# A graph layer in five stages: one block with a wait per engine in place of a barrier per stage, and one product placed ahead of a turn

## The reference, cut to what matters

```python
xn = _layernorm(x, axis=-1)
x = x + _L0_gnn_ref(xn, edge_index, ...) + _L0_mix_ref(xn[None], ...)[0]
x = x + _L0_ffn_ref(_layernorm(x, axis=-1)[None], ...)[0]
```

```python
phi_q = jnp.exp(jnp.einsum('bhnd,md->bhnm', q, rf) - q_norm)
phi_k = jnp.exp(jnp.einsum('bhnd,md->bhnm', k, rf) - k_norm)
kv = jnp.einsum('bhnm,bhnd->bhmd', phi_k, v)
numerator = jnp.einsum('bhnm,bhmd->bhnd', phi_q, kv)
attn = numerator / jnp.maximum(denominator, 1e-06)
return out @ proj_w.T + proj_b
```

```python
h = (x @ W).reshape(N, H, C)
e = jax.nn.leaky_relu(al_s[src] + al_d[dst], NEG_SLOPE)
alpha = ex / (denom[dst] + 1e-16)
out = jax.ops.segment_sum(h[src] * alpha[:, :, None], dst, num_segments=N)
h = jax.nn.elu(_gat_layer(x, src, dst, W1, ..., concat=True))
out = _gat_layer(h, src, dst, W2, ..., concat=False)
```

## Time and profile before

| | us |
|---|---|
| median of three runs | 2076.1 |
| lowest, highest | 2069.36, 2077.42 |
| the profiled execution | 2073.2 |
| its span | 2071.3 |

### The profile page before, as it was taken

One profiled execution on the slowest core, in us unless ns is written; L12 is line 12 of the kernel. 1 busy time (PEld: TensorE's weight loads), 2 busy tenths in 40 slices (PEclk: granted clock), 3 DMA queues, 4 the chain that ended last, 5 costly groups with the idle time before them and its releaser, 6 DMA issues. The chain is left out here.

```text
span 2071.3 us, 32352 instructions
## 1 busy us (share of the span) xinstructions
PE 1986.8 (96%) x9933; PEld 1467.1 (71%) x9934; DVE 1167.3 (56%) x2548; ACT 447.5 (22%) x822; POOL 185.0 (9%) x181
## 2 busy tenths in 40 slices
PE   5999899998999999999999999999989999999998
PEld 3666666666648887888888755556646777777876
DVE  6666436662566654888888642266863334343343
ACT  3222221222002321222222200013321222122222
POOL 0000000000000000000000000010002323233232
PEclk9999999999999999999999999999987999999999
DMA  8000220002644442732424234544126888899654
GB/s 262 18 17 20 93 108 17 17 19 75 219 144 149 151 128 73 221 124 86 139 91 137 68 146 155 182 125 157 49 75 227 247 270 258 228 286 281 177 137 84
DMA packets 81191, 282.78 MB, mean 137 GB/s; under 512 B 11689, under 2 KB 32225, under 8 KB 71490
## 3 DMA queue, kind: packets, MB, share of 16 engines
q1 hardware_dynamic: 59138, 211.02, 30.5%
q0 software_dynamic: 14848, 56.18, 11.3%
q10 hardware_dynamic: 7104, 14.26, 2.0%
HBM read 217.43 MB, written 63.99 MB: 136 GB/s over the span
## 5 line engine op out<-in xcount | busy, mean ns | idle before, releaser
L1402 PE MATMUL gat_Z<-h_head,first_rest 125*125 125x256 f32 (+1 forms) x1600 | 354.4, 380 | 3.9 <-DVEq L1302 3.9
L1402 PEld LDWEIGHTS gat_Z<-h_head,first_rest 125*125 125x125 f32 x1600 | 297.1, 188 | 49.7 <-issue 4.2
L777 PE MATMUL mix_G<-mix_w,xnT 128*125 128x384 f32 x720 | 246.3, 493 | 3.3 <-PEq L387 2.0
L777 PEld LDWEIGHTS mix_G<-mix_w,xnT 128*125 128x125 f32 x720 | 134.2, 191 | 89.4 <-issue 8.1
L2423 DVE TENSOR_SCALAR ex_idS<-ex_ids 128x1 int32 x52 | 8.0, 153 | 211.4 <-DMA out_rows<-ex_y,ex_idS 211.4
L2510 PE MATMUL ex_PH<-ex_xT,w_and_experts 128*128 128x128 f32 x936 | 113.4, 281 | 1.8 <-issue 0.9
L2510 PE MATMUL ex_PH<-ex_xT,ex_w 128*128 128x128 f32 x936 | 110.9, 277 | 0.5 <-issue 0.2
L2510 PEld LDWEIGHTS ex_PH<-ex_xT,w_and_experts 128*128 128x128 f32 x936 | 108.8, 195 | 2.8 <-issue 2.8
L2520 PE MATMUL ex_PY<-w_and_experts,ex_hT 128*128 128x384 f32 x312 | 107.5, 494 | 0.7 <-ACT ex_hT L2457 0.5
L2520 PE MATMUL ex_PY<-ex_w,ex_hT 128*128 128x384 f32 x312 | 107.3, 494 | 0.8 <-ACT ex_hT L2457 0.6
L2510 PEld LDWEIGHTS ex_PH<-ex_xT,ex_w 128*128 128x128 f32 x936 | 106.5, 192 | 0.7 <-issue 0.7
(11 more groups left out here) (400 smaller groups left out, 3096.2 us busy)
## 6 DMA issues: line engine op xcount, KB each, us to landing
w_and_experts<-in_L_ffn_W SPq DMA_DIRECT2D x32, 1152.0 KB, 8.9
ex_w<-in_L_ffn_W SPq DMA_DIRECT2D x32, 1152.0 KB, 8.5
first_wide<-c_dram SPq DMA_DIRECT2D x40, 546.9 KB
h1T_dram<-gat_oT ACTq DMA_DIRECT2D x40, 250.0 KB, 2.0
mix_w<-in_L_mix_qkv_w SPq DMA_DIRECT2D x6, 1152.0 KB, 12.8
ct_dram<-mix_count_out SPq DMA_DIRECT2D x40, 157.0 KB, 2.1
mix_w_slice<-in_L_gnn_W SPq DMA_DIRECT2D x6, 1024.0 KB, 12.3
proj_w2s<-in_L_gnn_W SPq DMA_DIRECT2D x4, 1536.0 KB, 9.2
```

The source lines that it names most:

```text
L777: last = pe.matmul(G[c][:], xnT[:, k, t * P:(t + 1) * P], w[:, k, c, :], start=(k == 0), stop=(k == KD - 1))
L1402: last = pe.matmul(Z[b][j][:], wt[b][:, s, :], h[hd][0:P, s, j * HC:(j + 1) * HC + j], start=(s == 0), stop=(s == NT - 1))
```

## The change

The stages from the first mixing half to the second projection stand in one block. The barriers and the empty block between them are gone; where one engine needs another's work, a wait on a semaphore stands on that engine. Eight PSUM banks (`bank[j]`) are named once, and each stage uses views of them. Both mixing halves and their numerators become one function. The norm, routing and expert stages keep their own blocks.

Other edits come with it:

- SP starts the second half's weights as soon as the first half's q, k and v are out of PSUM, part by part, and the projection's weights likewise behind the second half; it starts the second half's W1 slices when the first half's numerators are made;
- `phiq` lies over the W1 slices;
- PE's wait for `kv` stands behind the features of the queries, ahead of `R`;
- in the projection, a turn of a tile in the first half of the nodes waits for all numerators but the last; only the second tile's product waits for the last one;
- DVE makes the next stage's weights of tile 0 right after the second tile sum of the last pair in the first layer, and leaves the slopes of tile 1 to the next stage; the bias row is waited for at the first normalisation, no longer ahead of the first scores;
- semaphores are given back by POOL in `gat1_phase` and at the start of `gat2_route_phase`;
- a class `SecondStart` holds what the second projection needs first. DVE makes `T1`, `S` and one difference before it normalises the last tile (`first_sums`), and PE makes the second projection's first product ahead of the aggregation's last turn (`first_product`). `T1` lies in space of `h` there, and ACT copies it to where it is needed later.

```diff
-def numerator(nc, cx, tag, half, rfT, qT, kv, attn, load_next):
...
-        block = st.enter_context(nc.Block(no_gpsimd_drain=True))
...
+    @block.sync
+    def _(sp):
...
+        for half in range(2):
+            if half:
+                sp.wait_ge(num, 4 + SUMS)
+            for k in range(KH):
+                row = (half * KH + k) * 128
+                sp.dma_start(ws[k], gnn_w1[row:row + 128, :]).then_inc(slice_loaded[k], 16)
...
+            for c, (done, evac) in enumerate(((q_done, q_evac), (k_done, k_evac), (v_done, v_evac))):
+                sp.wait_ge(done, NT * (half + 1))
+                sp.wait_ge(evac, NT * (half + 1))
+                if half == 0:
+                    load_second(sp, c)
+            if half == 1:
+                load_proj(sp)
...
+        def numerators(half):
+            pe.wait_ge(s_evac, PER * NT * (half + 1))
+            with pe.Fori(0, HH // 2) as i:
+                for b in range(2):
+                    for j in range(6):
+                        m, c = j // CH, j % CH
+                        pe.wait_ge(q_exped, i * 12 + (FEATS * half + 6 * b + j + 1))
+                        pe.matmul(F[j][:, 0:CHW[c]], rfT[:, m * 128:(m + 1) * 128],
...
+                pe.wait_ge(kv_copied, 2 * (half + 1))
+                for b in range(2):
+                    pe.wait_ge(q_exped, i * 12 + (FEATS * half + 6 * b + 12))
...
 def proj_phase
...
         def _(sp):
+            sp.wait_ge(num, 4 + SUMS)
...
             def turn(t):
                 b = t % 2
+                pe.wait_ge(num_used, 2 + SUMS - (1 if t < NT // 2 else 0))
...
+                    elif t == 1:
+                        pe.wait_ge(num_used, 2 + SUMS)
...
 def first_layer_phase
...
+            sp.wait_ge(wa2_step, 2 * KF)
             load_w(0)
...
+            pool.wait_ge(projected, 2 * NT)
+            pool.wait_ge(summed, 2 * NT)
             pool.memset(large[:], BIG).then_inc(consts, 1)
...
                 tile_of(n, c22, p5_done, 1, 1, Y5)
                 if n == PAIRS - 1:
-                    slopes()
+                    weights(0)
...
-                if n == PAIRS - 1:
-                    weights(0)
...
+            pe.wait_ge(summed, 2 * NT)
             first(0)
...
 def gat1_phase
...
         def _(sp):
+            sp.wait_ge(p3_done, PAIRS)
             sp.dma_start(brow[:], b1.partition_broadcast(128)).then_inc(b_loaded, 16)
...
+            pool.wait_ge(p3_done, PAIRS)
+            cx.release(done_with)
...
-            dve.sem_inc(mn_ready, 2)
+            step(dve.scalar_tensor_tensor(u, u, SLOPE, u, ALU.mult, ALU.max))
             dve.tensor_tensor(e[1], u, rows[0][0:P, 1:2, P:2 * P].to_broadcast([P, NT, P]), ALU.subtract
                               ).then_inc(e_ready, 1)
-            dve.wait_ge(b_loaded, 16)
...
+                    if last and t == NT - 1:
+                        second.first_sums(dve)
                     normalise(hd, t)
...
+            pe.wait_ge(m_copied, 3)
+            pe.wait_ge(x_kept, 3 * PAIRS)
+            pe.wait_ge(ones_set, H1)
             aggregate(0, 0)
...
                     elif not last:
                         aggregate(hd + 1, 0)
+                    else:
+                        second.first_product(pe)
                     turn(hd, t)
...
 def gat2_project_phase
...
+            sp.wait_ge(turned1, H1 * NT + 2)
+            sp.wait_ge(t_evac1, H1 * NT + 2)
             load_pair(1)
...
+            dve.wait_ge(t1_kept, 1)
             dve.tensor_tensor(T4, B(1, 0), T2, ALU.subtract).then_inc(t_ready, 1)
...
+            act.wait_ge(t_ready, 1)
+            act.wait_ge(done, H1 * NT + 2)
+            act.activation(T1[:], second_start.T1, ACT.Copy).then_inc(t1_kept, 1)
...
+            pe.wait_ge(turned1, H1 * NT + 2)
             for n in range(HT):
-                first(n)
+                if n >= 1:
+                    first(n)
                 second(n)
...
+class SecondStart:
...
+    def first_sums(self, dve):
+        dve.wait_ge(self.ext_ready, 2)
+        dve.wait_ge(self.w_loaded, 128)
+        dve.tensor_tensor(self.T1, self.B(0, 1), self.B(0, 0), ALU.subtract).then_inc(self.t_ready, 1)
+        dve.wait_ge(self.first_loaded, 32)
+        dve.tensor_tensor(self.S, self.A(1, 0), self.A(1, 1), ALU.add).then_inc(self.s1_ready, 1)
+        dve.wait_ge(self.s1_ready, 1)
+        dve.tensor_tensor(self.A(1, 0), self.A(0, 0), self.A(1, 0), ALU.subtract).then_inc(self.s3_ready, 1)
+
+    def first_product(self, pe):
+        pe.wait_ge(self.ext_ready, 2)
+        pe.wait_ge(self.w_loaded, 128)
+        pe.wait_ge(self.first_loaded, 32)
+        for k in range(self.KH):
+            last = pe.matmul(self.bank[0:P, 0:self.W], self.A(0, 0)[:, k * P:(k + 1) * P], self.B(0, 0)[:, k, :],
+                             start=k == 0, stop=k == self.KH - 1, skip_group_check=True)
+        last.then_inc(self.x_done, 1)
...
+                bank = [pb(nc, st_b, f"bank{j}", [128, 512])[:] for j in range(8)]
+                block = st_b.enter_context(nc.Block(no_gpsimd_drain=True))
...
-            cx.clear()
```

752 lines of the change are left out of this document (383 added, 369 removed).

## The result

The changed kernel took **2049.7 us** (median of 4 runs, 2044.2 to 2054.7) against 2076.7 for the kernel before beside it (4 runs): ratio 0.988, 95% interval 0.9856 to 0.9904. The forecast was 2048. The profiled execution took 2047.5 us, and its span is 2045.7 (2071.3 before).

What follows compares the result with a forecast made beforehand. PE, busy for 96% of the span, was taken as the bound, so only its idle time and slow clock could pay; seven joints sum to 25.9 us off 2073.2, giving 2047.3, forecast 2048, with a range of 2042 to 2055.

Steps and rivals of the forecast that it cites:

- A: First half's last key and value sums to first `R`: idle 1.97 and slow clock 1.77 go, gain 3.74 us.
- B: First half's numerators to the second half: PE's wait of 2.03 and slow clock of 1.80 go, gain 3.83 us.
- D: Numerators to the projection: products start 1.52 earlier and 1.29 of slow clock goes, gain 2.81 us.
- C: Second half's last sums to its first `R`: same code as the first joint, gain 3.74 us, bounds 1.97 and 3.74.
- first rival: The slow clock stays, made by waits inside the stage; only idle time is won, 2059 us; chance 0.20.
- E: Projection to first layer: W1's load is issued 0.56 earlier, gain 0.56 us, bounds 0 and 1.97.
- F: First layer to aggregation: tile 0's weights come early, DVE is late next; gain 4.1 us, bounds 3.4 and 4.3.
- G: Aggregation to second projection: first product before the last turn, second product 7.1 us earlier; lower bound 4.0.
- The second: Rival: the gaps at joints are the price of entering a stage's code, not of the barrier; 2067 us, chance 0.05.
- The third: Rival: the expert loop of 52 turns gets slower because its code moved; 2098 us, chance 0.04.
- The fourth: Rival: the waits take the barriers' place, each engine's last work being what the next needs; 2074 us, chance 0.03.

Runs made afterwards that it cites:

- kv_first: Changed kernel with PE waiting for DVE's copy of the key and value sums ahead of the query features, both halves; 2054.25 us, ratio 0.9914 to the kernel before.
- division_first: Changed kernel with PE waiting for DVE's last division before the second half's first products and all projection turns; 2052.8 us, ratio 0.9916 to the kernel before.
- before_fill: Kernel before, barriers kept, with five unread products in each half's last tile; 2069.4 us against 2073.9, ratio 0.9975.
- fill_only: Changed kernel with five unread products in each half's last tile; 2045.0 us, ratio 0.9873 to the kernel before.
- repeat: The changed kernel run and profiled again, unedited; 2048.05 us, ratio 0.9871 to the kernel before.
- late_start: Changed kernel with the second projection's first sums and first product put back behind the last turn, without a barrier; 2059.2 us, ratio 0.9923 to the kernel before.

## Why the prediction was right

The sum held, in part by luck. Five of its seven steps held for the reasons given, one gave nothing and one was mis-sized.

**A, B, D.** Idle time and the slow clock behind it went together: 3.90, 3.92 and 2.70 for 3.74, 3.83 and 2.81. kv_first and division_first put the waits back and got idle times of 1.38 to 1.56, so DVE's late copy or division was the greater part of each gap. In before_fill the barrier's gap by itself brought the slow clock.

**C was the step that failed**: "The first joint again, same code: 3.74". The gap went there too, but its gain was 0.51 and -0.40. What came in its place is the first rival's mechanism, at this one joint: the last tile's idle places bring the clock down, and with the gap gone it stays low over sums (3.73 for 2.03) and features (10.36 and 11.27 for 8.60). fill_only shows what brings it down. In the kernel before the clock fell in that tile as well, but was back at 474.5, ahead of the last sums (476.08), so the slow features there came behind the barrier's gap alone, as the step had it. That the same code gives 10.3 at joint A and over 13 at joint C goes with how late the clock falls in the last tile; the runs don't settle what sets that.

**E was mis-sized**: 0.56 against 1.38 and 2.04. From the projection's second tile on, the load's issue gained about what the step said, 0.51 (it comes 76.91 behind that tile before, 76.40 in both profiles). The load's own time, which the step held fixed, is what differed. From its issue to DVE's first use it took 9.61 in the kernel before:

```profile
615.28 0.96 DVE L987 TENSOR_TENSOR first_rest<-first_rest 128x768 f32<-128x768 f32 x1 [5.31 <-DMA first_rest<-in_L_gnn_W]
```

In the profile after it took 8.92 (590.32 to 599.24), and W1 is late next, as the step had it: PE waits 0.59. In the repeat it took 7.94:

```profile
604.28 0.96 DVE L1000 TENSOR_TENSOR first_rest<-first_rest 128x768 f32<-128x768 f32 x1 [4.60 <-DMA first_rest<-in_L_gnn_W]
```

There W1 is not late, and PE wins all of its 1.97: from the attention rows to the sixth product it takes 16.65 without a wait (16.64 before, 605.72 to 622.36). Over the ten profiles with the load issued at this place it took 7.8 to 10.6, and PE's wait runs from none to 2.30. The three above 10 are those with work in the last tiles; why isn't known.

**F** gained 4.46 and 4.43 for 4.1, above the step's upper end of 4.3. The two waits of 0.71 and 0.29 were foreseen as under 1 and about 1: from one tile's weights to the next DVE takes 9.39 (797.47 to 806.86), where the step's chain has 9.74. No run takes this edit back, so F rests on the trace alone.

**G** gained 7.7 for 7.1. DVE's early sums delayed nothing, as worked out. late_start puts 6.2 of its gain and its sequel's, 7.6, down to the order.

**Why the sum hit in spite of C.** This is the luck in it. In the profile after the gain at C is 3.2 short, and 4.5 at the start, chance by the repeat, stands against it; routing and experts lost 2.5, where profiles of all kernels scatter between 689 and 697. In the repeat C is 4.1 short, and E, G and the last stage make up 3.4. The medians' difference of 27.0 us (23.7 in the repeat's comparison) lies about both profiles' 25.6 and 24.1, within the runs' scatter.

**The rivals.** The second fell: PE still branches into the loop of numerators, and its first features begin with no idle time (234.33). The page "Runtime: NRT & Kernel Launch" of the Trainium skill, section "Instruction fetch mechanics", has a taken branch out of the fetched stretch stop the engine; at this joint the trace shows no such stop. That doesn't contradict the page, as no row shows whether the branch left that stretch. The third fell: routing and experts took 694 and 690 us, 692 before. The fourth fell: no wait of the old size took a barrier's place, and what kept C's gain away was the clock.

## What to carry to other kernels

A barrier cost the late engine's time, the barrier itself, and at four of the five joints A to E the slow clock behind the gap; put the next stage's first product that needs nothing late into the last wait of the stage before. A loop's last turn, which has no next turn to fill its waits, can cost as much as a barrier: 4.3 us at joint C, gone with three products of the next stage in its place. Read a joint in several executions before giving it a price, and look at what runs there next to see that it isn't late in turn.

## What the runs showed of the hardware

- Gaps of 1.38, 1.51 and 1.54 us left the clock high behind them at the ends of the mixing halves, each in one execution; gaps of 1.97 to 2.03 there lowered it each time, at three joints in two executions (the kernel before and before_fill). That alone decides nothing: 1.71 lowered it at one joint, and 1.97 didn't at another.
- PE's idle places in one tile, in the profile after 0.23, 0.57, 0.68, 0.90 and 0.35 long, brought the lower clock, and with one more of 0.69 behind them it stayed low through products without a gap: there from before 462 until after 470. With the places filled it stayed at 1.00.
- Where the clock fell at most 9.8 us behind the ninth tile's sums, it was back before the last sums (9 of 9); where it fell 10.1 us or more behind them, it stayed low into the features (8 of 8).
- The same code, in two executions, took 11.85 and 14.69 us for its first 36 products.
- A load of W1, issued at the same place, was in use 7.94 and 8.92 us later in two executions of one kernel, and 9.61 in the kernel before; what waits for it can't be priced from one profile.
